# Attention scores and side matmuls in blocks of 32 columns, with a new table of side work and gathers of six transfers

## The reference, cut to what matters

```python
def poincare_fully_connected(x, z, r, c):
    lam = 2.0 / (1.0 - c * jnp.sum(x * x, axis=-1, keepdims=True))
    z_norm = jnp.maximum(jnp.linalg.norm(z, axis=0), EPS)
    inner = x @ (z / z_norm)
    v = 2.0 * z_norm * arcsinh(lam * inner * cosh(2 * r) - (lam - 1.0) * sinh(2 * r))   # c = 1
    w = jnp.sinh(v)
    return w / (1.0 + jnp.sqrt(1.0 + jnp.sum(w * w, axis=-1, keepdims=True)))
Q = poincare_fully_connected(x, z_q, b_q, C)
K = poincare_fully_connected(x, z_k, b_k, C)
V = x @ w_v.T + b_v
scores = jnp.einsum('bhqd,bhkd->bhqk', Qh, Kh) / np.sqrt(D_K)    # 16 heads of 16 features
probs = jax.nn.softmax(scores, axis=-1)
out = jnp.einsum('bhqk,bhkd->bhqd', probs, Vh)
```

## Time and profile before

| what | value |
|---|---|
| time, median of 3 runs | 3177.55 us (3175.37 to 3177.95) |
| the profiled execution's own time | 3171.44 us |
| its span, first to last instruction | 3169.6 us |
| granted TensorE clock, mean | 0.962 of 2.4 GHz |
| TensorE matmul busy in the span | 2838.4 us (90%) |
| ScalarE busy | 2026.5 us (64%) |
| VectorE busy | 1846.0 us (58%) |
| GpSimd busy | 1273.0 us (40%) |
| part B, first matmul to last | 1331.5 to 2773.4 us |
| exponentials of scores, L1859 | 1024, 1002.8 us busy |
| score matmuls, L1956 | 2048 records, 591.2 us busy |
| weighted sums, L1938 | 4096 records, 549.0 us busy |

### The profile page before, as it was taken

The page is one execution under the profiler, slowest core; times in us unless marked ns, Lnnn a source line. Parts: engine busy times, 40 slices in busy tenths (PEclk is TensorE's granted clock), DMA queues, the critical chain, the costliest instruction groups (busy, mean ns, idle before and its releaser), DMA issues. The chain is left out here.

```text
span 3169.6 us, 38539 instructions
## 1 busy us (share of the span) xinstructions
PE 2838.4 (90%) x12161; PEld 1226.5 (39%) x12161; DVE 1846.0 (58%) x2420; ACT 2026.5 (64%) x2650; POOL 1273.0 (40%) x786
## 2 busy tenths in 40 slices
PE   3899999999979999657999999999999999969997
PEld 1455555555554444322323232323233332234443
DVE  8899999999973453454443444444444441144444
ACT  6454555455425555325889797978878889835554
POOL 4798899889861220141314131322313230021210
PEclk7899999999999999778999999999999999989999
DMA  2010001010012211206263635535553627231112
GB/s 80 1 37 27 30 26 36 23 33 26 24 56 75 80 53 53 67 11 132 29 146 42 134 54 94 93 73 92 92 94 58 116 46 128 27 114 48 60 53 67
DMA packets 163998, 200.30 MB, mean 63 GB/s; under 512 B 16504, under 2 KB 118272, under 8 KB 163840
## 3 DMA queue, kind: packets, MB, share of 16 engines
q1 hardware_dynamic: 163840, 198.25, 28.4%
HBM read 139.49 MB, written 58.72 MB: 63 GB/s over the span
## 5 line engine op out<-in xcount | busy, mean ns | idle before, releaser
L1859 ACT ACTIVATE b_pr<-b_ps 128x1024 f32<-128x1024 f32 x1024 | 1002.8, 1025 | 255.5 <-PE b_ps L1956 251.2
L1956 PE MATMUL b_ps<-b_st 128*128 128x512 bf16 x2048 | 591.2, 386 | 71.0 <-DMA b_st<-b_scratch 31.6
L1938 PE MATMUL b_acc<-b_pr,b_vaug 128*32 128x512 f32 x4096 | 549.0, 608 | 0.4 <-ACT b_pr L1859 0.4
L1956 PEld LDWEIGHTS b_ps<-b_st 128*128 128x128 bf16 x2048 | 150.3, 98 | 649.5 <-ACT b_pr L1859 381.9
L1257 PE MATMUL f_po<-f_s,f_w 128*128 128x512 f32 x768 | 355.0, 605 | 9.4 <-DVE f_xr L1042 5.9
L1030 DVE TENSOR_TENSOR f_turned<-f_cs,f_s 128x1024 f32<-128x1024 f32 x96 | 119.3, 1243 | 364.4 <-ACT f_cs L1159 359.4
L635 PE MATMUL a_pv<-a_xnT,a_wv 128*128 128x512 f32 x512 | 251.2, 614 | 52.8 <-DVE a_mem L403 38.7
L1123 ACT ACTIVATE f_h<-f_po,f_b 128x512 f32<-128x512 f32 x192 | 131.9, 687 | 218.1 <-PE f_po L1257 218.1
L627 PE MATMUL a_pu<-a_xnT,a_wk 128*128 128x512 f32 x512 | 238.3, 609 | 29.2 <-DVE a_frac L355 23.2
L1575 POOL TENSOR_TENSOR b_SQ<-b_A 128x1024 f32<-128x1024 f32 x32 | 64.7, 2021 | 467.1 <-DVE b_A L1672 467.1
L674 PE MATMUL a_py<-a_wo,a_out 128*128 128x256 f32 x960 | 229.1, 382 | 0.0
(11 more groups left out here) (259 smaller groups left out, 4694.4 us busy)
## 6 DMA issues: line engine op xcount, KB each, us to landing
b_st<-b_scratch SPq DMA_DIRECT2D x512, 128.0 KB, 7.0
b_scratch<-b_parts SPq DMA_DIRECT2D x32, 768.0 KB, 7.7
f_xl<-x SPq DMA_DIRECT2D x16, 1024.0 KB, 5.5
f_xr<-x SPq DMA_DIRECT2D x16, 1024.0 KB, 6.8
a_xl<-in_L_attn_a_x_dram SPq DMA_DIRECT2D x16, 512.0 KB, 4.2
x<-a_xr SPq DMA_DIRECT2D x32, 256.0 KB, 2.2
x<-f_xr SPq DMA_DIRECT2D x8, 1024.0 KB, 4.5
b_xl<-x SPq DMA_DIRECT2D x8, 1024.0 KB, 7.8
```

Source lines behind the costliest of these rows:

```text
L1859: nc.scalar.activation(pr[:, 4 * (blk % 2) + j, :], ps[:, j % 2, :], ACT.Exp, scale=SC).then_inc(S["probs_done"], 1)
L1938: x = nc.tensor.matmul(acc[32 * j:32 * j + 32, h * 512:(h + 1) * 512], vaug[:, kt, c:c + 32], pr[:, 4 * (kt % 2) + j, h * 512:(h + 1) * 51 ...
L1956: x = nc.tensor.matmul(ps[:, j % 2, h * 512:(h + 1) * 512], st[:, g % 2, 1, j, kt * P:(kt + 1) * P], st[:, g % 2, 0, j, h * 512:(h + 1) * ...
```

## The change

- The scores (L1956 before) are made in four matmuls of 32 columns of keys each, into 32 rows of `ps` each, by a new helper `blocks`, in place of one of 128 columns. So are `lamb`, `facb`, `proj`, `v` and `sum`. The transposes (`inT`, `out`) stay at 128.
- A `proj` is cut in two: `proja` (k = 0) and `projb` (k = 1), behind different units. The steps of two tiles are now steps of one tile each (`inT` 0 to 3, `lamb` 0 and 1, `facb` 0 to 3, `out` 0 to 7). Each step has a fourth number in the table, the unit j that it stands at; `UNIT_OF` is gone.
- The table is new. `stats`, `rstd`, `lam`, `inT`, `lamb` and the first `proj` are done for the batch two ahead (offset 2); so `PROLOGUE` also does these for batch 1. The output of group 3 is made in block 7 of the next batch, not 2. `lamb` has its own diagonal `dgl`.
- The features of queries and keys are in the order (feature, head) within a group of four heads, by a permuted copy `zp` of the weights that ScalarE makes once, and biases loaded in eight small transfers. `b_scratch` then has the four heads of a feature in one run of 8 KB, and a gather is 6 transfers of 48 or 32 rows of 8 KB. The first query part is read once for three places.
- SyncE loads the next batch's input at the top of the batch.

```diff
-Q_PART = [0, 0, 0, 1, 1, 1, 2, 2]
-K_PART = [0, 1, 2, 0, 1, 2, 0, 1]
+Q_RUNS = [(0, 3, 0), (3, 3, 1), (6, 2, 2)]
+K_RUNS = [(0, 3, 0), (3, 3, 0), (6, 2, 0)]
...
-    3: [("lamb", 0, 1)], 4: [("proj", 0, 1), ("proj", 1, 1), ("vaug", 3, 0)], 5: [("proj", 2, 1)], 6: [("square", 0, 1), ("proj", 3, 1)],
...
-    7: [("root", 0, 1), ("y", 0, 1), ("v", 0, 1)], 8: [("ln", 0, 1), ("square", 1, 1), ("proj", 4, 1)],
...
+    4: [("square", 1, 1, 0), ("ln", 0, 1, 2), ("proja", 5, 1, 0), ("vaug", 3, 0, 0), ("projb", 5, 1, 2)],
+    5: [("root", 1, 1, 0), ("up", 0, 1, 2), ("proja", 6, 1, 0), ("y", 1, 1, 0), ("projb", 6, 1, 2)],
...
+    20: [("pair", 1, 1, 0), ("sum", 1, 1, 2)], 21: [("fac", 0, 1, 0)],
+    22: [("facb", 0, 1, 0), ("facb", 1, 1, 2)], 23: [("facb", 2, 1, 0), ("split", 0, 1, 0)], 24: [("facb", 3, 1, 0)],
...
+    [(step[:-1], int(step[-1]), 1) for step in "inT0 inT1 inT2 inT3 lamb0 lamb1 proja0 projb0".split()]
+TILE_KINDS = ("inT", "lamb", "projb", "v", "sum", "facb", "out")
+PE_KINDS = TILE_KINDS + ("proja",)
+ACT_KINDS = ("square", "root", "ln", "up", "down")
...
-    scratch = nc.dram_tensor("b_scratch", [2, 3, D, T], BF16, kind="Internal").ap()
+    scratch = nc.dram_tensor("b_scratch", [2, 3, H // 4, DK, 4, T], BF16, kind="Internal").ap()
...
-            for o, part in enumerate((Q_PART, K_PART)):
-                for i, w in enumerate(part):
-                    sp.dma_start(st[i * DK:(i + 1) * DK, slot, o],
-                                 scratch[o, w, 64 * g:64 * g + 64, :].rearrange("(h d) t -> d h t", d=DK))\
-                        .then_inc(st_loaded[slot], 16)
+            for i, n, w in Q_RUNS:
+                sp.dma_start(st[i * DK:(i + n) * DK, slot, 0].rearrange("p h t -> p (h t)"),
+                             scratch[0, w, g].rearrange("d h t -> d (h t)").unsqueeze(0).broadcast_to([n, DK, 4 * T]))\
+                    .then_inc(st_loaded[slot], 16)
+            for i, n, w in K_RUNS:
+                sp.dma_start(st[i * DK:(i + n) * DK, slot, 1].rearrange("p h t -> p (h t)"),
+                             scratch[1, w:w + n, g].rearrange("w d h t -> w d (h t)")).then_inc(st_loaded[slot], 16)
...
+                    if left > 1:
+                        sp.wait_ge(S["inT_done"], b + 2)
+                        sp.sem_inc(passed, 1)
+                        sp.dma_start(xl[:], dram(xi, b + 2)).then_inc(S["xl_loaded"], 16)
...
+                nc.scalar.activation(zp[:].rearrange("p o k (g d j) -> p (o k g) d j", g=G, d=DK),
+                                     z_sb[:].rearrange("p o k (g j d) -> p (o k g) d j", g=G, d=DK), ACT.Copy).then_inc(S["z_done"], 1)
...
-                        steps = [x for x in steps_at(blk, first, left) if x[0] in ("square", "root", "ln", "up", "down")]
                         for j in range(4):
-                            for kind, i, off in steps[j // 2:j // 2 + 1] if j % 2 == 0 else ():
-                                step(kind, i, b + off)
+                            for kind, i, off, at in steps_at(blk, first, left):
+                                if kind in ACT_KINDS and at == j:
+                                    step(kind, i, b + off)
                             n = 4 * BLK * b + 4 * blk + j
...
+                def blocks(o, w, v, start=True, stop=True):
+
+                    for r in range(0, P, 32):
+                        x = nc.tensor.matmul(o[r:r + 32], w[:, r:r + 32], v, start=start, stop=stop, skip_group_check=True)
+                    return x
...
+                    if kind in ("proja", "projb"):
+                        k = 0 if kind == "proja" else 1
+                        if k == 0:
+                            bank_free(m)
+                            if i == 0:
+                                pe.wait_ge(S["misc_taken"], m - 2)
                         q, c = i // 2, slice((i % 2) * 512, (i % 2 + 1) * 512)
-                        for k in range(KD):
-                            x = nc.tensor.matmul(bank, z_sb[:, q // 2, k, (q % 2) * P:(q % 2 + 1) * P], xnT[:, k, c],
-                                                 start=k == 0, stop=k == KD - 1)
+                        x = blocks(bank, zp[:, q // 2, k, (q % 2) * P:(q % 2 + 1) * P], xnT[:, k, c], k == 0, k == KD - 1)
+                        if k == 0:
+                            return
...
-                                x = nc.tensor.matmul(ps[:, j % 2, h * 512:(h + 1) * 512],
-                                                     st[:, g % 2, 1, j, kt * P:(kt + 1) * P],
-                                                     st[:, g % 2, 0, j, h * 512:(h + 1) * 512], start=True, stop=True)
+                                x = blocks(ps[:, j % 2, h * 512:(h + 1) * 512], st[:, g % 2, 1, j, kt * P:(kt + 1) * P],
+                                           st[:, g % 2, 0, j, h * 512:(h + 1) * 512])
...
-                            for q, (kind, i, off, h) in enumerate(tiles):
-                                if UNIT_OF[len(tiles)][q] == j:
+                            for kind, i, off, at in steps_at(blk, first, left):
+                                if kind in PE_KINDS and at == j:
                                     if kind == "out":
-                                        out(G * (b + off) + i, m - h, par - h, h)
+                                        out(G * (b + off) + i // 2, m, par, i % 2)
                                     else:
-                                        step(kind, i, b + off, m, par, h)
-                                    m, par = m + 1, par + 1
+                                        step(kind, i, b + off, m, par)
+                                    if kind in TILE_KINDS:
+                                        m, par = m + 1, par + 1
```

More of the change, by code:

```diff
@@ new lines @@
+    9: [("up", 1, 1, 0), ("v", 1, 1, 0)],
+    10: [("square", 3, 1, 0), ("v", 2, 1, 0), ("stats", 0, 2, 0)],
+    11: [("down", 1, 1, 0), ("v", 3, 1, 0), ("rstd", 0, 2, 0)],
+    12: [("ln", 2, 1, 0), ("v", 4, 1, 0), ("sign", 1, 1, 0)],
+    13: [("root", 3, 1, 0), ("v", 5, 1, 0), ("y", 3, 1, 0), ("out", 0, 0, 2), ("lam", 0, 2, 0)],
+    14: [("up", 2, 1, 0), ("v", 6, 1, 0), ("pair", 0, 1, 0), ("out", 1, 0, 2)],
+    15: [("down", 2, 1, 0), ("v", 7, 1, 0)], 16: [("ln", 3, 1, 0), ("sum", 0, 1, 0), ("sign", 2, 1, 0)], 17: [("up", 3, 1, 0)],
@@ L1372, in steps_at @@
+TILE_KINDS = ("inT", "lamb", "projb", "v", "sum", "facb", "out")
+PE_KINDS = TILE_KINDS + ("proja",)
+ACT_KINDS = ("square", "root", "ln", "up", "down")
 def steps_at(blk, first, left):
-    return [(kind, i, off) for kind, i, off in STEPS.get(blk, [])
-            if off <= left and not (first and (kind, i) in (("out", 3), ("vaug", 3)))]
+    return [(kind, i, off, at) for kind, i, off, at in STEPS.get(blk, [])
+            if off <= left and not (first and (kind, i) in (("out", 6), ("out", 7), ("vaug", 3)))]
@@ L1409, in phase_b @@
         dg = s.sb("dg", [P, 2, NT, P])
+        dgl = s.sb("dgl", [P, NT, P])
         A = s.sb("A", [P, 4, T])
@@ L1432, in phase_b, with misc_base @@
         st_loaded = [s.sem(f"st_loaded{i}") for i in range(2)]
[L1433 to L1444 removed]
+        N_W = 16 * 12
+        N_G = 16 * (len(Q_RUNS) + len(K_RUNS))
+        PRO = sum(kind in TILE_KINDS for kind, _, _ in PROLOGUE)
+        offs = [off for blk in range(BLK) for kind, _, off, _ in STEPS.get(blk, []) if kind in TILE_KINDS]
+        TILES, LATE = len(offs), offs.count(-1)
+        AHEAD, LAST = offs.count(2), offs.count(1) + offs.count(2)
+        assert TILES % 2 == 0
+        def misc_base(b, first=False, left=2):
+            skipped = 0 if first else LATE + (AHEAD if left == 0 else 0)
+            return (PRO - skipped + TILES * b, (PRO - skipped) % 2)
         def store_parts(sp, b, f):
@@ L1599, in batch @@
                     for blk in range(BLK):
-                        for kind, i, off in steps_at(blk, first, left):
+                        for kind, i, off, _ in steps_at(blk, first, left):
                             step(kind, i, b + off)
@@ L1813, in _ @@
                     take_acc(G * B - 1, h)
-                m, par = misc_base(B, False)
-                out(G * B - 1, 3, B - 1, m - LAST, par + LAST)
+                m, par = misc_base(B, left=0)
+                for h in range(2):
+                    out(G * B - 1, 3, B - 1, m - LAST + h, par + LAST + h, h)
             @block.scalar
@@ L1943, in batch @@
                 def batch(b, first=False, left=2):
-                    m, par = misc_base(b, first)
+                    m, par = misc_base(b, first, left)
                     for blk in range(BLK):
                         g, kt = blk // NT, blk % NT
-                        tiles = [(kind, i, off, h) for kind, i, off in steps_at(blk, first, left)
-                                 for h in range(N_TILES.get(kind, 0))]
                         if kt == 0:
@@ L1985, in _ @@
                 for kind, i, off in PROLOGUE:
-                    for h in range(N_TILES.get(kind, 0)):
```

(5 more changed lines are left out.)

178 lines of the change are left out of this document (82 added, 96 removed), and 10 rows, old and new, of tables (PROLOGUE, STEPS).

## The result

| | before | after |
|---|---|---|
| time, median (range), us | 3176.46 (3174.16 to 3177.95) | 3267.91 (3263.22 to 3271.8) |
| ratio, 95% interval | | 1.0288 (1.027 to 1.0306) |
| profiled span, us | 3169.6 | 3267.2 |
| loop batches 2 to 4, start to start, us | 172.4 to 173.4 | 178.9 to 179.1 |
| first exponential of the attention, us | 1449.0 | 1475.1 |

The changed kernel is 91 us slower where 92 us faster was forecast. I read the stretches of two batches first, those of the earlier trace rows. Columns: stretch, its length, then busy time (and instructions) of PE, PEld, DVE, ACT, POOL, the granted clock, the DMA share, GB/s.

The account below looks back on a forecast made before the run. TensorE was taken to set the pace, ScalarE 14% behind, with a two-buffer score ring bounding quiet blocks. Batch savings of 94.4, less 4.4 and 1.5, plus 4.0 at the start, gave 92.5 us: 3085 us, range 3064 to 3124.

Parts of the forecast that it names:

- TensorE's times (1, 2): Scores and side matmuls in 32-column blocks: a pair 0.87, a weighted sum 0.86, a TensorE block 3.46 us, sum tiles 1.0.
- A: Rival: a start-up at each group of 32-column score blocks stays, 0.28 us a block, giving 3122 us; 12%.
- D: Rival: bf16 column blocks run one after another, scores 4 times as long, 32 x 5.2 us a batch more; 1%.
- C: Rival: TensorE cannot be fed its loads and matmuls, at 64 ns each 780 us more, 3950 us; 3%.
- The rule and the table (3, 4): A block takes the largest of TensorE's sum, ScalarE's sum and the two-buffer loop; new table 154.8 for 166.6 us a batch.
- the ring: Attention block's dependency loop through only two score buffers, scores to exponentials to weighted sum: 4.25 us before, 4.01 forecast.
- 6 x 11.8 + 15.1 - 4.4 - 1.5: Six batches' savings plus the second last's, less slow clock after four jumps (4.4) and factor broadcast waits (1.5), in us.
- The last batch: Final batch with hardly any side work, bound by the score-buffer loop: 138.3 to 129.8, 8.5 us saved.
- The factor broadcast: From block 20's second sum to the broadcast in block 22, TensorE waits 0.2 us a batch: 7 x 0.2 = 1.5.
- The queues (6): SP's transfers: store 7.7 and gather 16.7 us fit the 25.5 before the next batch by 1 us; no cost.
- Rival B: A side chain or the gather arrives late each batch by 4 us: 8 x 4 = 32 less gain, 3117 us; 8%.
- The start (7): Before batch 0: faster gather against added setup and prologue work, net -1 to +8 us of gain, 4 taken.

Follow-up runs that it names:

- x1: Changed kernel with a gather of 16 transfers again, one per 16 destination partitions, still in rows of 8192 bytes; 3088.39 us, ratio 0.9738.
- x3: Changed kernel with the gather as before the change: 16 transfers in pieces of 2048 bytes, scratch padded behind each row; 3089.27 us, ratio 0.9722.
- x5: Kernel before with only the six-transfer gather and its scratch layout, permuted weight columns and bias loads; 3326.64 us, ratio 1.0492.
- x7: x1 with scores and side matmuls back at the full 128 columns, so the new table without the blocks; 3156.04 us, ratio 0.9944.
- x6: Kernel before with only the scores and side matmuls in four blocks of 32 columns; 3160.91 us, ratio 0.9968.
- x11: x6 with the six-transfer gather of x5; 3287.75 us, ratio 1.036.
- x4: Changed kernel with 11 transfers a gather: keys in three of 48 or 32 flat rows, queries in eight of 16 rows; 3078.67 us, ratio 0.9707.
- x9: Changed kernel with a gather of two transfers to 128 partitions in flat 8192-byte rows, query copies made by the stores; 3091.81 us, ratio 0.9739.

## Why the prediction was wrong, step by step

**TensorE's times (1, 2): right.** Block starts in the changed kernel, in a quiet block and around a sum:

```profile
2112.89 1.03 PE L1963 MATMUL b_acc<-b_pr,b_vaug 128*32 128x512 f32 x8
2113.82 0.62 PE L1897 MATMUL b_ps<-b_st 128*32 128x512 bf16 x8
2114.26 0.72 PE L1897 MATMUL b_pm<-b_cst,b_A 128*32 128x1 f32 x64
2114.84 0.61 PE L1897 MATMUL b_ps<-b_st 128*32 128x512 bf16 x8
2115.28 1.04 PE L1963 MATMUL b_acc<-b_pr,b_vaug 128*32 128x512 f32 x8
2116.13 1.06 PE L1897 MATMUL b_ps<-b_st 128*32 128x512 bf16 x16
2117.02 1.03 PE L1963 MATMUL b_acc<-b_pr,b_vaug 128*32 128x512 f32 x8
```

A weighted sum to the next scores is 0.85 to 0.86 (2115.28 to 2116.13; forecast 0.86, before 0.99). A pair to the weighted sum is 0.89 (2116.13 to 2117.02; forecast 0.87, before 0.97). A sum of 64 records takes 0.58 to 0.60 where I had 1.0, and before 1.70. A passage around transposes is 0.25 (0.22). Rivals A and D fall with these rows. So does C: the 64 matmuls of a sum start within 0.55 us (2114.26 to 2114.81), 9 ns apart, and their loads beside them, where it wanted over 35 ns for each load or matmul. The bf16 loads of 32 columns, which the trace of before did not have, take 0.09 us each and lie under the matmuls.

**The rule and the table (3, 4): right.** ScalarE's exponentials of blocks 20 and 21:

```profile
2112.74 3.79 ACT L1878 ACTIVATE b_pr<-b_ps 128x1024 f32<-128x1024 f32 x4 [0.35 <-PE b_ps L1897]
2116.87 3.77 ACT L1878 ACTIVATE b_pr<-b_ps 128x1024 f32<-128x1024 f32 x4 [0.35 <-PE b_ps L1897]
2120.90 1.02 ACT L1878 ACTIVATE b_pr<-b_ps 128x1024 f32<-128x1024 f32 x1 [0.26 <-PE b_ps L1897]
```

Block 20 takes 4.13 us (forecast 4.46, with its sum at 1.0; 4.06 with the measured 0.6), block 21 4.03 (forecast 4.01; the ring of before 4.25). In x1 the block medians are 5.7, 5.1, 5.3 for blocks 1 to 3 (5.18), 5.5, 5.7, 5.6 for 4 to 6 (5.91), 4.6 to 4.9 for most of 7 to 17 (4.84), 4.3 for 23 and 24 (4.32). From the first exponential of batch 0 to that of batch 7, x1 takes 1105.5 us and before 1185.5: 80.0 less. The steps for these seven gave 6 x 11.8 + 15.1 - 4.4 - 1.5 = 80.0. The last batch with the end has 10.1 for 8.5. The factor broadcast waits 1.6 us in 7 for 1.5. That 80.0 is met to the decimal is luck in part: x1's blocks 4 to 6 are 0.2 to 0.4 us shorter than the rule, its block 10 is 0.6 longer, and its waits for issue are 22.1 us in all where before had 17.1. (The old table puts two ScalarE steps in seven blocks, not six; the sum of 166.6 has all seven.)

**The queues (6): this step failed.** Its chain and its place, the first scores of each batch, were right: in x3, with a gather of the old speed, TensorE waits for one only twice, 6.7 us in all. Its price was not. It took the gather at 16.7 us, "as slow as today's", and for the start "anything from 6 to 17 us", "with 6 transfers and long rows". I had read from the trace how fast a transfer of today's shape is, and carried this to another shape as if fewer and longer could only help. The bounds of an operation that the trace doesn't show had to reach above today's as well. Nor had I read the DMA share of a gather alone (0.98, above), which shows that today's is spread over all engines, and a source that now began with 3 was in the diff. By 3 engines of 8192 bytes in 0.31 us it comes to 4 x 16 + 2 x 16 = 96 rows on the first engine, 29.8 us, 13 more than 16.7. Measured from first to last packet, the gathers of the changed kernel take 30.5 to 36.6 us, one 40.0; the one issued at 2146.11 slows down from 2174 on, while the next input's load moves.

**Rival B was the mechanism** at 4 us a batch and 8%. Measured, a batch costs 19.6 us more than in x1: (1242.4 - 1105.5) / 7, with 15 to 19 of waiting at block 0, 3 at block 8, and the half clock behind. In the last batch, whose blocks have no side work, blocks 8 and 16 wait 10.6 and 5.8 us more, and it is 24.9 us longer than x1's.

**The start (7): wrong in sign.** I took 4 us of gain, range -1 to 8. x1's first exponential is 6.7 us later than before's. The setup costs 5.0 us (x5), of which I had 0 to 3, and the rest of the start another 4 to 5 (x7: 10 later in all). The blocks alone bring it 2.9 earlier (x6). In the changed kernel the slow gather makes it 26.0 later.

**The sum.** From x1 to the changed kernel the spans differ by 181.0 us: 19.3 at the start, 136.9 in seven batches, 24.9 in the last. x1 itself is 83 below before: 80.0 and 10.1 less, 6.7 more. Except for the start, the forecast described x1. The range was too narrow since only one of its cases, B, touched the gather, with a price that had no row behind it.

What stays open: why the new table, with about as many instruction loads a batch as x6 (18 for 19), mostly escapes the stop within a batch (x1 waits 22.1 us for issue, x6 43.8; x1's stops within a batch are two of 1.2 us). That the two edits are worth more together is measured, and that x6 loses to late instruction loads is shown by x11 for block 18. Why those loads fall better in the new order was not tried.

## What to carry to other kernels

When transfers are merged, write down the slowest dimension of both sides of each new one and read the DMA share in a stretch where it runs alone; share times 16 is the number of engines. A 3 in front left 13 of 16 DMA engines idle and turned a gain of 83 us (x1) into a loss of 91; flattening the key rows (48 in front, x4) gained 93. Take the parts of a change apart before judging it: here the one that was least argued for decided.

## What was unexpected of the hardware

- The rate of a gather goes by engines, and on the same engines it still differs by a factor of nearly 3. Two engines gave 56 GB/s, three 70 to 72, eight 124, sixteen 131 to 134 with transfers to 16 partitions each, 152 with keys to 48 and 32, and 359 with two flat transfers to 128. Rows of 2048 or 8192 bytes made no difference to the rate, but with three engines SP was held up far longer by the short ones (16.46 us for three transfers, against 2.09).
- TensorE's instructions come over the same DMA engines. With x6's gather of 16 transfers on all of them, a load of 16384 bytes took 1.65 us instead of 0.95 and came too late: 3.35 us of standstill within a group, and a clock of 0.55 over the next 6.5 us. With a gather on three engines (x11) block 18 had no such wait. At the loop's jump, where before had 17.1 us in 4, no run with free engines can tell, as TensorE waits there for the gather. In x9, whose gathers last 6 to 9 us, a load beside one took 0.9 to 1.2 us, and TensorE never stopped for 0.6 us or more within a loop batch.
- One-column fp32 matmuls in four blocks of 32 take 0.6 us for 8 token tiles, against 1.7 for 8 at the full width, 2.9 times as fast.
- SP's issue of a store right behind a gather on three engines took 14.15 us for two transfers (0.90 when nothing was queued); 12 stores behind one another took 15.3.
